# A graph-attention megakernel: first neighbour sweep inside the making of h, staggered tile pairs, scaling on ScalarE, mask conversion on GpSimd, weights loaded first

## The chip, the cores and the metric

The kernel runs on one core of a Trainium2 chip. The metric is device time in microseconds (us), here the median of three runs. TensorE is PE, VectorE is DVE, ScalarE is ACT, GpSimd is POOL, and SyncE (SP) issues most DMAs. An engine works through its own instructions in order and meets the others only through semaphores.

## The reference

Two graph layers follow each other, each with a residual and a layer norm, on x of 8 batches (B) x 2048 nodes (N) x 64 features (D); adj is a 2048 x 2048 matrix of 0 and 1.

```
h = einsum('bnf,of->bno', inp, W_w) + W_b ; h[:, 0] = 0
mask = (adj[1:, :] > 0)
neigh = einsum('ji,bjf->bif', mask, h[:, :N-1])
s = einsum('bif,fi->bi', h, a[:64]) + einsum('bif,fi->bi', neigh, a[64:]) ; s[:, 0] = 0
x1 = layernorm(x + leaky(s[:, :, None] * h.sum(1)[:, None, :]))
...
scores = where(adj + eye > 0, h1 @ h1.T, -1e16) ; softmax(scores) @ h1      (4 heads, then once more)
```

So the first layer needs one masked product over all nodes, and a scaling of each node; the second is dense attention, 8 x 4 instances of 2048 x 2048 in "layer 1" and 8 in "layer 2". The same adjacency serves both: as 0/1 for the product, and as 0/-1e16, with the diagonal at 0, for the attention.

## The kernel before

Everything is written out by hand with semaphores; each engine's program is its own function. Nodes go in 16 tiles (NT) of 128; one row of a tile holds 8 batches x 64 features = 512 columns. The part before the attention has these stages, in order:

- Loads. SP issues x in eight DMAs, then nine DMAs of weights and `a`, then two rows of adjacency tiles; the other adjacency tiles follow as their buffers come free.
- Weights. PE turns the weights and `a` (L642 to L651), DVE and ACT copy them out.
- Making of h, once per tile: POOL stages x (L570), PE transposes it (L661), ACT copies that (L893), PE multiplies it (L666), DVE adds the bias (L1024), takes the partial s (L1027, L1029), splits h into a high and a low part (L895 on ACT, L1032), and turns the adjacency integers into a 0/1 mask tile (L1036).
- The sum of h over all nodes: 32 matmuls (L673, L674), copied by ACT.
- Four neighbour sweeps on PE (L687, L688). A sweep makes 4 of the 16 output tiles in 4 PSUM banks from 16 x 4 x 2 matmuls of 512 columns. Tile 0 of the product uses a copy of h shifted by one node (`shifted`), which comes first in each sweep. Sweeps take turns on banks 0 to 3 and 4 to 7.
- Centring, on DVE, in pairs of tiles: eleven steps from the product (L1050) to the scaled result (L1086). In it DVE hands the centred values to ACT to be squared (L902), and the variance to POOL for the power -0.5 (L577), and waits for both before the scaling.
- Mask conversion on DVE: for each tile the diagonal (L1090) and then (m - 1) * 1e16 over 2048 columns (L1093).
- 32 units, each 4 tiles of one batch: POOL splits x1 (L586, L589), PE transposes (L704), ACT copies (L908), PE multiplies by the four heads (L724), ACT and DVE take the high and low parts (L920, L1103), PE turns them (L714), ACT and DVE copy (L913, L1098). SP stores `h_d` (L409) and `hT_d` (L413) to DRAM. A unit's buffers are those of the unit two before it, so L920 waits for that unit's store.
- Operand loads: SP waits for all stores, then loads the operands of attention instances 0 and 1 (L427, L423; 1.5 MB each). Then the attention starts (L819 on PE, L1160 on DVE).

The attention, from there to the end, is not touched by the change.

## Time and profile before

| what | value |
|---|---|
| median of 3 runs | 3358.05 us (3353.57 to 3359.98) |
| the profiled execution's own time | 3353.93 us |
| its span | 3352.2 us |
| PE, DVE, ACT, POOL busy | 91%, 83%, 70%, 75% |

The span is what the trace covers; 1.7 us lie around it. Busy shares are means over stages that are limited by different things, so the stages have to be read apart.

### The profile page before, as it was taken

Reading aid. Unit: us, or ns where it says so; the run is one execution under the profiler, and the core shown is the slowest. Engines: PE = TensorE matmul, PEld = TensorE weight load, DVE = VectorE, ACT = ScalarE, POOL = GpSimd, SP = SyncE. Lnnn points to the kernel's source line nnn. Section 1 sums busy time; section 2 is a strip of 40 time slices with the busy share of each in tenths; the row PEclk is TensorE's granted clock in tenths of the full one; section 3 lists DMA queues with packets and bytes.
Section 4 is the critical chain, followed back from the end, with each engine's and each line's share of the span. In section 5 each row is a group of like instructions: output and inputs, shape, how many; then the busy total and the mean of one; then the engine's idle time right before and its main releaser. Section 6 shows DMA issues by size and latency. Waiting matters only on the chain. (4 is left out here: it accounts for less than half of the span.)

```text
span 3352.2 us, 127058 instructions
## 1 busy us (share of the span) xinstructions
PE 3066.7 (91%) x49399; PEld 2295.4 (68%) x49399; DVE 2766.2 (83%) x5392; ACT 2336.7 (70%) x2678; POOL 2507.0 (75%) x1828
## 2 busy tenths in 40 slices
PE   3874599999999999999999999999996699999997
PEld 3433477777777777777777777777765577777775
DVE  5486488888888888888888888888876699999998
ACT  1104577777777777777777777777765588888886
POOL 1023189999999899999999999999986346676776
PEclk7887899999999999999999999999998899999998
DMA  5104879989999998999898899989966533333331
GB/s 205 66 0 150 285 134 164 164 154 170 167 156 161 165 164 157 161 166 161 156 170 166 156 163 167 161 158 174 163 124 209 189 123 125 118 135 119 134 120 73
DMA packets 1189157, 507.55 MB, mean 151 GB/s; under 512 B 1090718, under 2 KB 1148508, under 8 KB 1186588
## 3 DMA queue, kind: packets, MB, share of 16 engines
q1 hardware_dynamic: 1187564, 497.60, 69.9%
q8 instruction: 342, 5.60, 0.7%
q0 software_dynamic: 1200, 3.93, 0.3%
q14 instruction: 51, 0.42, 0.0%
HBM read 102.12 MB, written 62.91 MB: 49 GB/s over the span
## 5 line engine op out<-in xcount | busy, mean ns | idle before, releaser
L605 POOL TENSOR_TENSOR mask_slot<-probs 128x1024 f16<-128x1024 f32 x1024 | 1916.2, 1893 | 221.7 <-ACT probs L962 146.5
L962 ACT ACTIVATE probs<-scores,shifted_max 128x2048 f32<-128x2048 f32 x512 | 1026.1, 2004 | 177.0 <-DVE shifted_max L1165 172.9
L1160 DVE CUSTOM_DVE_ANT_0 scores<-ps,mask 128x1024 f32<-128x1024 f32 x512 | 625.8, 1222 | 206.6 <-PE ps L820 204.7
L819 PE MATMUL ps<-operands 128*128 128x512 f16 x2048 | 778.2, 380 | 12.4 <-DMA v_parts<-h_d 11.3
L820 PE MATMUL ps<-operands 128*128 128x512 f16 x2048 | 777.5, 380 | 0.0
L967 ACT COPY probsT<-ps 128x1024 bf16<-128x1024 bf16 x512 | 518.1, 1012 | 352.3 <-PE ps L828 352.3
L1160 DVE CUSTOM_DVE_ANT_0 scores<-ps,mask,neg_max 128x1024 f32<-128x1024 f32 x512 | 657.4, 1284 | 99.7 <-issue 52.8
L828 PEld LDWEIGHTS ps<-ident,probs 128*128 128x128 bf16 x8192 | 519.6, 98 | 291.9 <-issue 157.6
L828 PE MATMUL ps<-ident,probs 128*128 128x128 bf16 x8192 | 623.7, 219 | 5.8 <-DVE probsT L1169 3.6
L839 PE MATMUL ps<-v_parts,probsT 128*128 128x64 f16 x8192 | 548.0, 193 | 0.0
L838 PE MATMUL ps<-v_parts,probsT 128*128 128x64 f16 x8192 | 547.6, 193 | 0.0
L838 PEld LDWEIGHTS ps<-v_parts,probsT 128*128 128x128 bf16 x8192 | 512.5, 98 | 0.0
L839 PEld LDWEIGHTS ps<-v_parts,probsT 128*128 128x128 bf16 x8192 | 498.9, 98 | 0.0
L1169 DVE COPY probsT<-ps 128x1024 bf16<-128x1024 bf16 x512 | 354.0, 691 | 3.5 <-PE ps L828 3.4
L942 ACT ACTIVATE probsT<-ps 128x512 f16<-128x512 f32 x512 | 291.3, 595 | 78.1 <-PE ps L753 78.1
L811 PE MATMUL ps<-v_parts,probsT 128*128 128x64 f16 x8192 | 327.5, 193 | 15.7 <-DMA probsT<-mask_slot 9.9
L1129 DVE SCALAR_TENSOR_TENSOR probsT<-ps,probsT 128x512 f16<-128x512 f32 x512 | 329.4, 684 | 12.0 <-ACT probsT L942 3.5
L753 PE MATMUL ps<-ident,probs 128*128 128x128 f32 x2048 | 299.7, 279 | 5.8 <-DVE probsT L1129 4.7
L819 PEld LDWEIGHTS ps<-operands 128*128 128x128 f16 x2048 | 200.7, 98 | 136.6 <-DMA v_parts<-h_d 11.6
L811 PEld LDWEIGHTS ps<-v_parts,probsT 128*128 128x128 f16 x8192 | 276.0, 98 | 20.2 <-DMA probsT<-mask_slot 12.4
L820 PEld LDWEIGHTS ps<-operands 128*128 128x128 f16 x2048 | 200.7, 98 | 121.6 <-issue 1.1
L753 PEld LDWEIGHTS ps<-ident,probs 128*128 128x128 f32 x2048 | 226.7, 141 | 74.9 <-ACT probs L938 40.2
(169 smaller groups left out, 4545.2 us busy)
## 6 DMA issues: line engine op xcount, KB each, us to landing
mask_slot<-mask SPq DMA_DIRECT2D x129, 512.0 KB, 2.9
operands<-hT_d SPq DMA_DIRECT2D x40, 512.0 KB, 4.2
operands<-hT_d SPq DMA_DIRECT2D x80, 256.0 KB, 4.0
v_parts<-h_d SPq DMA_DIRECT2D x40, 512.0 KB, 4.6
scores<-in_adj SPq DMA_DIRECT2D x16, 1024.0 KB, 4.8
h_d<-probs SPq DMA_DIRECT2D x32, 512.0 KB, 3.5
hT_d<-probs SPq DMA_DIRECT2D x32, 512.0 KB, 2.8
probsT<-mask_slot SPq DMA_TRANSPOSE x1024, 3.5
```

The costliest lines, as they stand in the source:

```text
L605: pool.tensor_tensor(low[:, u, w], probs[:, u, w], high[:, u, w], ALU.subtract).then_inc(sem(f"low{half}"), 1)
L753: last = pe.matmul(ps[:, TURN_BANK[q], j * P:(j + 1) * P], probs[:, slot, c * P:(c + 1) * P], ident[:, :], start=(j == 0), stop=(j == 3), ...
L811: added = pe.matmul(out_slot(tt), lowT[:, u, c * P:(c + 1) * P], v_parts[:, held, c * P:c * P + D], start=False, stop=(c == NT - 1))
L819: pe.matmul(ps[:, b, :], hi_lo[:, p, t * P:(t + 1) * P], hi_lo[:, p, w], start=True, stop=False)
L820: scored = pe.matmul(ps[:, b, :], hi_lo[:, p, t * P:(t + 1) * P], lo_hi[:, p, w], start=False, stop=True)
L828: flipped = pe.transpose(high_bank(half)[:, j * P:(j + 1) * P], high[:, u, key:key + P], ident16[:, :])
L838: pe.matmul(out_slot(tt), w, v_parts[:, held, c * P:c * P + D], start=(c == 0), stop=False)
L839: added = pe.matmul(out_slot(tt), w, v_parts[:, held, c * P + D:(c + 1) * P], start=False, stop=False)
L962: act.activation(probs[:, 1 - u, :], scores[:, 1 - u, :], ACT.Exp, bias=shifted_max[:, 1 - u:2 - u], scale=-1.0, accum_out=row_sum[:, held ...
L967: act.copy(highT[:, u, N // 2:N], high_bank(1)).then_inc(sem("high_copied1"), 1)
L1160: dve.tensor_tensor_reduce(scores[:, u, w], ps[:, 2 * c:2 * c + 2, :].rearrange("p a n -> p (a n)"), mask[:, t * N + c * 2 * BANK:t * N + ...
L1169: dve.tensor_copy(highT[:, u, 0:N // 2], high_bank(0)).then_inc(sem("high_copied0"), 1)
```

## The change

Five edits, all ahead of the attention:

1. SP issues the nine weight DMAs before the eight of x.
2. PE's first sweep is spread over the making of h: the products of tile t-1 follow the making of h of tile t. The shifted tile now comes last in every sweep. The loops are written out.
3. DVE's pairs of tiles are staggered: the squares' sum and the variance of a pair are taken in the middle of the next pair. For this the centred values take turns between two buffers. The final scaling leaves DVE: ACT does it as eight activations of 64 columns for each tile (`normalize`).
4. The mask conversion goes from DVE to POOL, one tile after each second unit (`mask_step`); the diagonal is now a multiplication by `off_diagonal` after the conversion.
5. SP loads the operands of instance 0 before the last four units' stores, and those of instance 1 behind these stores; the waits for the stores move in part to ACT's first two exponentials.

```diff
@@ sync
-            for b in range(B):
-                sp.dma_start(xs[:, b * NT * D:(b + 1) * NT * D],
-                             x[b].rearrange("(p t) c -> p (t c)", t=NT)).then_inc(sem("x_loaded"), 16)
             sp.dma_start(w_nat[0:D, 0:D], w0).then_inc(sem("weights_loaded"), 16)
...
+            for b in range(B):
+                sp.dma_start(xs[:, b * NT * D:(b + 1) * NT * D],
+                             x[b].rearrange("(p t) c -> p (t c)", t=NT)).then_inc(sem("x_loaded"), 16)
...
+            with sp.Fori(0, B - 1) as b:
+                serve_units(b)
...
+            for u in range(2):
+                sp.wait_ge(sem(f"h_stored{u}"), 8 * (UNITS - NT // G))
+                sp.wait_ge(sem(f"hT_stored{u}"), 8 * (UNITS - NT // G))
+            for k in range(OPERAND_DMAS):
+                load_part(0, 0, k)
+            serve_units(B - 1)
+            for k in range(OPERAND_DMAS):
+                load_part(1, 1, k)
@@ gpsimd
-            units(pool, part_step)
+            def mask_step(t):
+
+                m = col(mask, t, N)
+                pool.tensor_scalar(m, m, -1.0, MASKED_SCORE, ALU.add, ALU.mult).then_inc(sem("mask_scaled"), 1)
+                pool.wait_ge(sem("mask_scaled"), t + 1)
+                gate(pool, "pool")
+                d = mask[:, t * (N + P):t * (N + P) + P]
+                pool.tensor_tensor(d, d, off_diagonal[:, :], ALU.mult).then_inc(sem("mask_ready"), 1)
+
+            for t in range(NT):
+                part_step(2 * t, 0)
+                part_step(2 * t + 1, 1)
+                mask_step(t)
@@ tensor
+            make_h(0, 0)
+            make_h(1, 1)
+            for t in range(2, NT):
+                make_h(t, t % 2)
+                products_of(0, 0, t - 1, t == 2)
+            products_of(0, 0, NT - 1, False)
...
+            products_shifted(0, 0, False).then_inc(sem("neigh_ready"), 1)
             pe.wait_ge(sem("hsum_copied"), 1)
...
+            for sweep in range(1, 4):
+                u = sweep % 2
+                if sweep >= 2:
+                    pe.wait_ge(sem("neigh_free"), 4 * (sweep - 1))
+                for t in range(1, NT):
+                    products_of(sweep, u, t, t == 1)
+                products_shifted(sweep, u, False).then_inc(sem("neigh_ready"), 1)
@@ scalar
+            def normalize(i):
+                sm = small[:, :, i % 2 * B:(i % 2 + 1) * B]
+                act.wait_ge(sem("a_rstd"), i + 1)
+                for b in range(B):
+                    scaled = act.activation(x_btc[:, b, i, :], pair(centred(i))[:, b, :], ACT.Copy, scale=sm[:, 3, b:b + 1])
+                scaled.then_inc(sem("x1_done"), 1)
@@ vector
+                if i0:
+                    for i in (i0 - 2, i0 - 1):
+                        spread(i)
+                    for i in (i0 - 2, i0 - 1):
+                        variance(i)
...
-                        dve.tensor_tensor(x_btc[:, :, i, :], pair(w[:, 2, :]), over(sm[:, 3, :]), ALU.mult).then_inc(sem("x1_done"), 1)
-
-            with dve.Fori(0, NT) as t:
-                d = mask[:, bass.ds(t * (N + P), P)]
-                dve.tensor_tensor(d, d, ident16[:, :], ALU.max).then_inc(sem("mask_diag"), 1)
-                dve.wait_ge(sem("mask_diag"), t + 1)
-                m = mask[:, bass.ts(t, N)]
-                dve.tensor_scalar(m, m, -1.0, MASKED_SCORE, ALU.add, ALU.mult).then_inc(sem("mask_ready"), 1)
```

On POOL, at the start of the units, before the change (L591 makes the bias rows, L586 and L589 split one unit's x1; the row behind the first four is the loop's branch):

```order
L591 COPY operands<-bh_rows 128x2048
L586 CAST scores<-xs 128x4x64
L589 TENSOR_TENSOR scores<-xs,scores 128x4x64
L586 CAST scores<-xs 128x4x64
L589 TENSOR_TENSOR scores<-xs,scores 128x4x64
L174 UNCONDITIONAL_BRANCH
```

The same place of the changed kernel (L602 and L605 are the split, L612 the conversion of one mask tile, L616 its diagonal):

```order
L607 COPY operands<-bh_rows 128x2048
L602 CAST scores<-xs 128x4x64
L605 TENSOR_TENSOR scores<-xs,scores 128x4x64
L602 CAST scores<-xs 128x4x64
L605 TENSOR_TENSOR scores<-xs,scores 128x4x64
L612 TENSOR_SCALAR mask<-mask 128x2048
L616 TENSOR_TENSOR mask<-mask,off_diagonal 128x128
L602 CAST scores<-xs 128x4x64
L605 TENSOR_TENSOR scores<-xs,scores 128x4x64
```

Two instructions on the mask now stand between each second unit and the next, 16 times over.

On PE, in the making of h, before the change (L661 transposes x, L666 multiplies it):

```order
L661 MATMUL ps<-ident,probsT 128x128 x4
L666 MATMUL ps<-w0T,outs 128x128 x4
L659 REGISTER_ALU
L661 MATMUL ps<-ident,probsT 128x128 x4
L666 MATMUL ps<-w0T,outs 128x128 x4
```

And of the changed kernel (L688 and L693 are the same two steps, L701 and L702 the products of the sweep with h's high and low part):

```order
L688 MATMUL ps<-ident,probsT 128x128 x4
L693 MATMUL ps<-w0T,outs 128x128 x4
L701 MATMUL ps<-probs,mask 128x512
L702 MATMUL ps<-operands,mask 128x512
L701 MATMUL ps<-probs,mask 128x512
L702 MATMUL ps<-operands,mask 128x512
L701 MATMUL ps<-probs,mask 128x512
L702 MATMUL ps<-operands,mask 128x512
L701 MATMUL ps<-probs,mask 128x512
L702 MATMUL ps<-operands,mask 128x512
L688 MATMUL ps<-ident,probsT 128x128 x4
L693 MATMUL ps<-w0T,outs 128x128 x4
```

Eight products of 512 columns now stand between two tiles' transposes.

## Rows read from the trace of the kernel before

**Rows 1.** Busy time in stretches: length, then engines, granted clock, DMA share, GB/s.
```profile
29.50:122.00 92.50, 50.32 (x225) 38.89 (x226) 72.53 (x80) 19.79 (x33) 13.47 (x15) 0.65 0.48 162
149.70:268.00 118.30, 82.78 (x384) 37.35 (x382) 95.11 (x193) 9.85 (x16) 25.96 (x16) 0.86 0.00 0
288.20:405.50 117.30, 74.82 (x868) 62.15 (x868) 58.41 (x65) 74.07 (x91) 28.77 (x54) 0.95 0.79 279
418.00:2555.00 2137.00, 2101.68 (x37028) 1565.90 (x37026) 1804.60 (x3727) 1601.47 (x1549) 1930.02 (x1030) 0.99 0.90 160
```

**Rows 2.** Timeline, loads' end and first tile: start, length, engine, line, idle before.
```profile
14.21 0.61 POOL L570 COPY probsT<-xs 128x512 f32 x1 [11.06 <-DMA xs<-in_x]
22.73 0.28 PE L642 MATMUL ps<-ident,scratch 64*64 64x64 f32 x1 [22.73 <-DMA rows<-in_L_gnn_beta]
29.58 1.00 PE L661 MATMUL ps<-ident,probsT 128*128 128x128 f32 x4 [2.44 <-ACT probsT L886]
...
31.25 2.08 PE L666 MATMUL ps<-w0T,outs 128*128 128x128 f32 x8 [0.68 <-ACT outs L893]
```

**Rows 3.** Timeline of the making of h.
```profile
55.57 1.16 PE L666 MATMUL ps<-w0T,outs 128*128 128x128 f32 x8 [2.09 <-ACT outs L893]
...
98.65 0.68 DVE L1024 TENSOR_TENSOR mask_slot<-ps,rows 128x512 f32<-128x512 f32 x1
...
100.72 2.08 PE L666 MATMUL ps<-w0T,outs 128*128 128x128 f32 x8 [2.09 <-ACT outs L893]
...
103.67 0.69 DVE L1024 TENSOR_TENSOR mask_slot<-ps,rows 128x512 f32<-128x512 f32 x1
```

**Rows 4.** Timeline of the four sweeps, first and last of 512 matmuls.
```profile
121.81 0.39 PE L687 MATMUL ps<-operands,mask 128*128 128x512 f16 x1 [1.20 <-ACT hsum L898]
...
232.10 0.38 PE L688 MATMUL ps<-operands,mask 128*128 128x512 f16 x1
```

**Rows 5.** Timeline of the end of the last pair's centring.
```profile
261.68 0.69 DVE L1075 SCALAR_TENSOR_TENSOR mask_slot<-small,mask_slot 128x512 f32<-128x512 f32 x1
...
264.09 3.24 POOL L577 TENSOR_TENSOR small<-small,half_neg 128x8 f32<-128x8 f32 x2 [11.52 <-DVE small L1082]
265.75 0.69 DVE L1086 TENSOR_TENSOR xs<-probsT,small 128x512 f32 x1 [1.80 <-POOL small L577]
267.36 0.69 DVE L1086 TENSOR_TENSOR xs<-mask_slot,small 128x512 f32 x1 [0.91 <-POOL small L577]
```

**Rows 6.** Timeline of the units' first and last steps, and the attention's first.
```profile
268.12 1.89 POOL L591 COPY operands<-bh_rows 128x2048 f32<-128x2048 f32 x1 [0.79 <-DVE xs L1086]
...
274.99 1.01 ACT L920 CAST probs<-ps 128x1024 f16<-128x1024 f32 x1 [1.98 <-PE ps L724]
...
288.23 2.35 DVE L1103 TENSOR_TENSOR probs<-ps,probs 128x1024 f16<-128x1024 f32 x2
...
400.69 1.22 DVE L1103 TENSOR_TENSOR probs<-ps,probs 128x1024 f16<-128x1024 f32 x1 [2.31 <-ACT probs L920]
...
402.66 1.86 PE L714 MATMUL ps<-ident_h,probs 128*128 128x128 f16 x16 [3.08 <-DVE probs L1098]
...
418.04 1.22 DVE L1160 CUSTOM_DVE_ANT_0 scores<-ps,mask 128x1024 f32<-128x1024 f32 x1 [12.79 <-PE ps L820]
```

**Rows 7.** Waits in the first 420 us: total, times, longest.
```profile
ACT probs L920 <- DMA h_d<-probs: 31.3, 26, 1.6
```

**Rows 8.** Groups of instructions by form: busy, mean ns, idle before.
```profile
L589 POOL TENSOR_TENSOR scores<-xs,scores 128x256 f16<-128x256 f16 x28 | 19.2, 685 | 5.1 <-POOL scores L586 5.1
...
L356 POOL TENSOR_SCALAR scratch<-outs 128x512 f32<-128x512 f32 x15 | 28.9, 1924 | 3.1 <-POOL outs L354 3.1
...
L354 POOL TENSOR_TENSOR outs<-outs,rows 128x512 f32<-128x512 f32 x15 | 19.1, 1277 | 2.7 <-POOL outs L353 2.7
...
L951 ACT ACTIVATE outs<-ps 128x64 f32 x93 | 20.8, 223 | 19.6 <-PE ps L767 19.6
...
L340 POOL TENSOR_SCALAR stats<-stats 128x8 f32<-128x8 f32 x30 | 5.9, 198 | 5.8 <-POOL stats L334 5.8
```

More of the change, by code:

```diff
@@ L63, in build @@
         ident16 = sb("ident16", [P, P], BF16)
+        off_diagonal = sb("off_diagonal", [P, P], BF16)
         ident_h = sb("ident_h", [P, P], F16)
@@ new lines, in products @@
+            def products(sweep, u, t, hi, lo, start, stop):
+                for j in range(4):
+                    m = mask[:, t * N + sweep * (4 * P) + j * P:t * N + sweep * (4 * P) + (j + 1) * P] if isinstance(t, int) else \
+                        mask[:, bass.ds(t * N + (sweep * (4 * P) + j * P), P)]
+                    pe.matmul(ps[:, 4 * u + j, :], m, hi, start=start, stop=False)
+                    last = pe.matmul(ps[:, 4 * u + j, :], m, lo, start=False, stop=stop)
+                return last
@@ new lines, in products_of, with products_shifted @@
+            def products_of(sweep, u, t, start):
+                pe.wait_ge(sem("mask_made"), t + 1)
+                if sweep == 0:
+                    pe.wait_ge(sem("lo_made"), t)
+                products(sweep, u, t, col(h_hi, t - 1, BD), col(h_lo, t - 1, BD), start, False)
+            def products_shifted(sweep, u, start):
+                return products(sweep, u, 0, shifted[:, 0:BD], shifted[:, BD:2 * BD], start, True)
+            make_h(0, 0)
[3 more added lines that the diff above has]
+                products_of(0, 0, t - 1, t == 2)
@@ L1095, in copy_hT @@
+            for i in (NT - 2, NT - 1):
+                spread(i)
+            for i in (NT - 2, NT - 1):
+                variance(i)
             def copy_hT(k, u):
```

169 lines of the change are left out of this document (79 added, 90 removed).

## The prediction

> **What bounds the kernel now.** I first read busy times by stretch [rows 1]. From 418 to 2555 us is the first attention layer, PE busy 2102 of 2137 us; the change does not touch it, nor what follows. All edits fall before 418 us, so the question is by how much the first attention step, DVE's L1160 at 418.04 [rows 6], moves. Then I read the timeline at each junction there, asking which engine has no gaps. In the making of h, DVE is busy 72.5 of 92.5 us while PE is at clock 0.65 on average [rows 1]; a tile takes DVE 5.02 us, from one L1024 to the next [rows 3]. The four sweeps run without a gap: 511 steps in 110.3 us, 0.216 us each, 27.6 us a sweep [rows 4]. DVE can't start centring before the first is through, then needs 118.3 us for 8 pairs, 14.8 each [rows 1], so the other three hide behind it. In the units no engine is full; ACT's L920 waits 31.3 us in 26 times for a store [rows 7], and a unit takes 117.3 / 32 = 3.67 us [rows 1]. POOL has 28.8 us of work there, in 54 instructions, so 1.07 us a unit [rows 1].
>
> I write times on the clock of the trace before.
>
> **Weights first.** x lands at 14.2, all weights at 22.7; PE then needs 6.9 us for weights and `a` before the first transposes at 29.6 [rows 2]. With the weights in front, their chain runs while x still arrives, and the start hangs on x: POOL's copy, 0.61, then PE. x is there at 22.7 at the latest (before, everything had landed by then): transposes at 23.4, gain 6.2. At best the weights, a third of x's bytes or less, cost 3.5 us more than x's 14.2: gain 11. I take x at 20.5, gain 8.3.
>
> **First sweep in the making of h.** In order, PE now does transposes of t, waits for ACT's copy, multiplies, then does 8 products of tile t-1 once DVE has made that mask tile, which is at the end of its 5.02 us. At full clock, from then on: 8 x 0.216 = 1.7, transposes at most 1.0 and the copy 0.68 [rows 2], multiplication 1.16 [rows 3]: 4.6 us, below 5.02, so DVE stays the bound and the products cost nothing. The cover is 0.4 us thin. At half the clock (L666 2.08 in place of 1.16 [rows 3]) it is 3.45 + 1.0 + 0.68 + 2.08 = 7.2 us, and 0.2 of handing over: 2.4 us more a tile. PE starts there cold; I charge 2 us for the first such tile, and expect full clock after, since PE would be over nine tenths busy at the half clock and 70% at the full one, while the units' stage holds 0.95 with 74.8 of 117.3 us busy, 64% [rows 1].
>
> The last mask tile is made at 103.67 + 2 x 5.02 = 113.7 [rows 3]. Then 8 products (1.7), the 32 matmuls of the sum of h (6.9) and 8 products of the shifted tile (1.7): DVE can start at 124.1 instead of 149.7. With 8.3 gained above and 2 paid: 117.9.
>
> **Staggered pairs.** A pair loses the two waits for POOL, 1.80 and 0.91 [rows 5], the two scalings (start to start 0.60 each) and about 0.2 of waiting for the square: 14.8 becomes 10.7. Two pairs, 21.4 us, now fit under a sweep of 27.6, so PE bounds: 117.9 + 3 x 27.6 = 200.7. Behind the last sweep come two pairs, 21.4, to 222.1. What is late next is the tail: from the end of the last L1075 (262.37) to the end of the powers (267.33), 5.0 us [rows 5], then ACT's eight scalings of the last tile at 0.223, the nearest row (L951, out of PSUM [rows 8]): 1.8. ACT's other scalings hide under DVE's pairs: 16 x 0.223 + 2 x 0.63 = 4.8 of 10.7 us. x1 is complete at 228.9, against 268.05 before: 39 us gained.
>
> **Mask conversion on POOL.** DVE loses the wait till 288.23 for L1103, whose input was there at 276.0 (L920, 274.99 + 1.01) [rows 6]. POOL gets, after each second unit, one TENSOR_SCALAR with two operations over 2048 columns. No row has this in bf16. The nearest is L356, the same instruction with two operations, 512 columns in 1.924 us, and L340 with 8 columns in 0.198 [rows 8]: 1.726 / 504 = 3.42 ns a column, so 0.2 + 2040 x 0.00342 = 7.2 us. From below it is bounded by the copy of 2048 columns, 1.89 [rows 6]; from above by twice the slowest two-input rate, L354, (1.277 - 0.198) / 504 = 2.14 ns, twice that over 2040 columns: 8.9. I take 7.2: same engine, same form. L356 repeats at 1.92 in 15 places, so no neighbour makes it slow. With the diagonal (0.45; 256 columns take 0.685 [rows 8]) and a wait of 0.18, a mask step is 7.8 us, and a round of two units and a mask tile 2 x (1.07 + 0.18) + 7.8 = 10.3 us. The units want 2 x 3.67 = 7.3. **So POOL becomes the bound of this stage**, behind it PE's L704, which waits for the split, and everything after. This eats most of the gain.
>
> POOL starts 1.96 after x1 is complete (L591 ends at 270.01 [rows 6]): 230.9. The split of unit 30 ends at 230.9 + 15 x 10.3 + 1.25 = 386.7, the last mask tile at 395.7. From the split of unit 30: 4.6 to its L1103 (as at the first unit: 276.1, less 271.5 for the split's end), 3.7 to that of unit 31, 3.8 to the end of L714 (400.69 to 404.52 [rows 6]), 2.2 to DVE's first step (four matmuls and the start), and 1.5 for a cold PE: 15.8. L1160 starts at 402.5 in place of 418.04.
>
> **Operands early.** The 12.8 us for which DVE waited before L1160 [rows 6] go; that is in the line above. In the units SP loads 1.5 MB more, at 279 GB/s [rows 1] 5.4 us; in rounds of 10.3 us there is room for it. ACT's waits for the last stores fall into the first steps of the attention; behind them are only exponentials whose inputs are not yet there.
>
> **Sum.** 418.0 - 402.5 = 15.5 us off the profiled execution's own 3353.9: 3338.4. That execution lies 4.1 below the median of 3358.05, so a median could be 3342.5. I predict 3341.
>
> **Rivals.**
>
> *POOL's conversion is quick, and all the gain stays.* From a mask instruction of 4.2 us down, the round is under 7.3 and the stage keeps its 3.67 a unit. Then L1103 starts at 228.9 + 8.0 = 236.9, that of unit 31 at 236.9 + 31 x 3.67 + 1.5 = 352.2, and SP's early loads now do cost their 5.4 (nothing at least; up to 9, when the wait for the landed stores adds to it): 357.6; 6.0 on to L1160: 363.6, a gain of 54.4: 3299.5 to 3303.7. For it: L591, 2048 columns with one input in 1.89. Against it: L356, and that its minimum is no obviously dearer operation than an addition. Chance 0.22. The Trainium skill (GPSIMD Engine Reference, Engine selection) says that one-input elementwise work is roughly at line rate on GpSimd; by that the conversion would take about what L591 takes, and this rival would be the result. L356 in this trace disagrees with it, and I go by the trace.
>
> *In between*, 4.2 to 6.4 us an instruction: each microsecond is 16 us of time, 3304 to 3328. Chance 0.14.
>
> *TensorE stays at half clock while h is made* (slower). Place: PE between two mask tiles. Price 2.4 us x 14 tiles = 34 us, less the 2 charged: 3341 + 32 = 3373. It takes 9 cold tiles to turn my forecast into a loss above 0.2%. For it: the clock is 0.65 in this stage now [rows 1]. Against it: PE's share rises well over what the units' stage holds its clock with. Chance 0.07.
>
> *POOL's conversion is dearer than L356 tells*, bf16 in and out costing more: from 8.6 us on the kernel is slower by more than 0.2%; at 8.9 it is 3368. Chance 0.07.
>
> My forecast, 6.4 to 8 us, has 0.50; its own range is 3328 to 3354.
>
> **How the numbers follow.** 0.2%, 6.7 us, is about what a measurement of this kernel can tell from no change. The two upper cases hold 0.14, the lower ones 0.36; a range of 3297 to 3358 leaves out most of the upper two and the very bottom. Faster: 0.22 + 0.14 and all but the upper edge of the forecast, 0.78. Within 0.2%: an instruction of 7.8 to 8.6 us, or a few cold tiles: 0.11. Slower: 0.11.
>
> **What would show it.** After: the first transposes near 21 us; DVE's centring starting near 118, PE's three sweeps without a gap, DVE waiting for them; x1 complete near 229. Then POOL without gaps through the units, the mask's TENSOR_SCALAR at 7.2, rounds of 10.3, PE's L704 waiting for POOL, L1160 near 402. Wrong if that instruction is under 4.2 us (then the stores bound the units, and L1160 is near 364), or if granted clock in the making of h stays near 0.5 and DVE waits for PE there.

## The result, and the profile after

The changed kernel took 3320.16 us (median of 4 runs, 3313.20 to 3323.41); the kernel before took 3355.81 beside it (4 runs). The ratio is 0.9888, with a 95% interval of 0.9872 to 0.9903: about 36 us less, where the prediction had 17. The profiled execution took 3323.41 us, of which 3321.7 are its span. DVE's first attention step, `tensor_tensor_reduce` of the scores, is now L1217 (it was L1160 [rows 6]; L1160 now is the remainder of a unit, which was L1103). It moved from 418.04 to 375.22, by 42.8 us; the prediction had it at 402.5.

Busy time of the changed kernel in the stretches that answer to [rows 1]: length, then the engines, granted clock, DMA share, GB/s.

```profile
25.10:119.00 93.90, 64.42 (x310) 39.41 (x311) 75.71 (x80) 20.69 (x32) 15.15 (x15) 0.85 0.49 169
128.90:232.00 103.10, 82.73 (x384) 37.30 (x382) 80.62 (x172) 33.48 (x121) 27.63 (x14) 0.92 0.00 1
249.00:370.00 121.00, 74.05 (x851) 61.10 (x852) 55.84 (x61) 73.05 (x92) 64.89 (x89) 0.94 0.77 269
```

The third row is the one to read first. The prediction made POOL the bound of the units; it is busy 64.9 of 121 us there. This is the row of the mask's instruction (count, shortest/median/longest in ns, first and last start), and under it POOL's timeline through one round of two units and a mask tile:

```profile
L612 POOL TENSOR_SCALAR mask<-mask x16: 1895/1897/1899, 245.8 to 351.8; 128x2048 bf16<-128x2048 bf16 x16
```
```profile
285.80 1.90 POOL L612 TENSOR_SCALAR mask<-mask 128x2048 bf16<-128x2048 bf16 x1
287.88 0.43 POOL L616 TENSOR_TENSOR mask<-mask,off_diagonal 128x128 bf16<-128x128 bf16 x1 [0.18 <-POOL mask L612]
288.25 0.40 POOL L602 CAST scores<-xs 128x256 f16<-128x256 f32 x1
...
291.93 0.40 POOL L602 CAST scores<-xs 128x256 f16<-128x256 f32 x1 [2.43 <-PE ps L744]
...
293.14 1.90 POOL L612 TENSOR_SCALAR mask<-mask 128x2048 bf16<-128x2048 bf16 x1
```

1.90 us and not 7.2. A round takes 293.14 - 285.80 = 7.3 us, which is what two units want, and POOL waits 2.4 us of it for PE.

The start. Timeline of the changed kernel at the loads' end (answers to [rows 2]), then its first 24 us in two stretches (columns as above):

```profile
13.86 0.28 PE L670 MATMUL ps<-ident,scratch 64*64 64x64 f32 x1 [13.86 <-DMA rows<-in_L_gnn_beta]
24.37 0.61 POOL L587 COPY probsT<-xs 128x512 f32 x1 [20.82 <-DMA xs<-in_x]
25.13 1.09 PE L688 MATMUL ps<-ident,probsT 128*128 128x128 f32 x4 [6.91 <-POOL probsT L587]
```
```profile
2.00:14.00 12.00, 0.14 (x1) 0.13 (x1) 0.17 (x1) 0.14 (x1) 1.33 (x6) 1.00 0.61 181
14.00:24.40 10.40, 4.21 (x23) 3.39 (x22) 3.77 (x10) 2.05 (x4) 0.03 (x1) 0.83 1.03 421
```

The weights are there 9 us earlier, but x 10 us later. The first transposes gain 29.58 - 25.13 = 4.4 us, where 8.3 were predicted: while the weights come, DMA moves 181 GB/s, and x only then runs at 421.

The centring. DVE's last mask tile and its first centring step (answers to [rows 4]), then the end of the centring and the first unit (answers to [rows 5, 6]):

```profile
114.84 1.86 DVE L1090 TENSOR_SCALAR mask<-scores 128x2048 int32 x1
128.86 0.69 DVE L1114 TENSOR_TENSOR probsT<-ps,probsT 128x512 f32<-128x512 f32 x1 [12.16 <-PE ps L702]
```
```profile
234.06 0.69 DVE L1101 TENSOR_REDUCE small<-probsT 128x8 f32<-128x512 f32 x1 [1.81 <-ACT probsT L952]
...
235.49 3.23 POOL L593 TENSOR_TENSOR small<-small,half_neg 128x8 f32<-128x8 f32 x2 [4.14 <-DVE small L1106]
237.16 3.93 ACT L943 ACTIVATE xs<-outs,small 128x64 f32<-128x64 f32 x16 [2.62 <-POOL small L593]
241.15 1.89 POOL L607 COPY operands<-bh_rows 128x2048 f32<-128x2048 f32 x1 [2.42 <-ACT xs L943]
248.98 1.23 DVE L1160 TENSOR_TENSOR probs<-ps,probs 128x1024 f16<-128x1024 f32 x1 [13.44 <-ACT probs L972]
```

Centring starts 20.9 us earlier than before (31.9 predicted), x1 is complete at 241.1, 27 us earlier (39 predicted), and the first remainder of a unit 39.3 us earlier: the other 12 us come from DVE, which no longer stands before it with the mask.

The end of the units. SyncE's timeline, and ACT's and DVE's there:

```profile
356.54 1.90 SPq L435 DMA_DIRECT2D operands<-hT_d  x3
358.50 0.56 SPq L431 DMA_DIRECT2D v_parts<-h_d  x1
359.12 0.42 SPq L415 DMA_DIRECT2D h_d<-probs  x1
```
```profile
366.51 1.01 ACT L972 CAST probs<-ps 128x1024 f16<-128x1024 f32 x1 [9.20 <-DMA h_d<-probs]
...
371.04 1.22 DVE L1160 TENSOR_TENSOR probs<-ps,probs 128x1024 f16<-128x1024 f32 x1 [1.66 <-ACT probs L972]
...
375.22 1.22 DVE L1217 CUSTOM_DVE_ANT_0 scores<-ps,mask 128x1024 f32<-128x1024 f32 x1 [0.43 <-PE ps L860]
```

The new place of a cost: SyncE loads instance 0 ahead of the last four units' stores, and ACT waits 9.2 us for one of these. From the first remainder to the last it takes 122.1 us, 9.6 more than before (288.23 to 400.69 [rows 6]). In return DVE no longer waits 12.8 us before the attention.

Theory: the mechanism was right, and the price of one instruction, the mask conversion, was wrong; two smaller sizes (the start, and the making of h with the sweep inside) were wrong on the other side. Rival: the mask's price matters little, because something else (buffers between POOL and PE, transfers) sets the units' pace anyway; and the gain comes from other edits.

### The profile page after: what moved, and what is told of

It is laid out like the page before. It is cut to its first block and busy times, and to the rows that moved or that the text cites. A ratio compares the mean times of both kernels' runs of the same rounds, so it can differ in the third digit from the quotient of the medians.

```text
span 3321.7 us, 126248 instructions
## 1 busy us (share of the span) xinstructions
PE 3065.0 (92%) x49399; PEld 2287.0 (69%) x49399; DVE 2739.8 (82%) x5344; ACT 2369.3 (71%) x2806; POOL 2546.0 (77%) x1861
## 5 line engine op out<-in xcount | busy, mean ns | idle before, releaser
L1217 DVE CUSTOM_DVE_ANT_0 scores<-ps,mask 128x1024 f32<-128x1024 f32 x512 | 625.5, 1222 | 202.4 <-PE ps L860 196.5
L1217 DVE CUSTOM_DVE_ANT_0 scores<-ps,mask,neg_max 128x1024 f32<-128x1024 f32 x512 | 657.3, 1284 | 103.4 <-issue 57.7
L851 PEld LDWEIGHTS ps<-v_parts,probsT 128*128 128x128 f16 x8192 | 275.7, 98 | 25.9 <-DMA probsT<-mask_slot 21.0
```

Of the source, the lines that this page charges most:

```text
L851: added = pe.matmul(out_slot(tt), lowT[:, u, c * P:(c + 1) * P], v_parts[:, held, c * P:c * P + D], start=False, stop=(c == NT - 1))
L1217: dve.tensor_tensor_reduce(scores[:, u, w], ps[:, 2 * c:2 * c + 2, :].rearrange("p a n -> p (a n)"), mask[:, t * N + c * 2 * BANK:t * N + ...
```

## The experiments

Stage times below are starts of the first attention step unless said otherwise; in the changed kernel it is 375.2, and 375.6 in a second profile of it (`a0_after_again`, below), so differences are taken to 375.4. Apart from the changed kernel and `c2_together`, every variant was executed once.

**What made the nearest row dear.** Ahead of POOL's wait for x, seven instructions by themselves:

```diff
+            for o, i, c1, c2, op1, op2 in ((wide, wide, -1.0, 2.0, ALU.add, ALU.mult), (wide, wide, 0.0, -0.8, ALU.min, ALU.mult),
+                                           (flat, src, -1.0, 2.0, ALU.add, ALU.mult), (flat, src, 0.0, -0.8, ALU.min, ALU.mult),
+                                           (flat, src, 0.0, -0.8, ALU.max, ALU.mult), (flat, src, -0.8, None, ALU.mult, None),
+                                           (flat, src, 0.0, None, ALU.min, None)):
```

> The changed kernel, and ahead of it, while GpSimd has nothing to do but wait for x, seven TENSOR_SCALAR on GpSimd over buffers that are rewritten later: two over 2048 bf16 columns (add then multiply; minimum then multiply) and five over 512 fp32 columns (add, multiply; minimum, multiply; maximum, multiply; multiply alone; minimum alone). The mask's instruction took 1.897 us for 2048 bf16 columns, the row that I had priced it from, minimum and multiply over 512 fp32 columns, 1.924. Theory A, the minimum is what is slow: 2048 bf16 with minimum about 7 us, 512 fp32 with add about 0.5 us and with minimum 1.9. Theory B, fp32 is what is slow: both wide bf16 ones 1.9 us, all two-operation fp32 ones 1.9. Theory C, it was slow because VectorE worked at the same time: all of 512 columns near 0.5 us here, where VectorE is idle.

The seven in their order (L593 is the call with one operation; count, shortest/median/longest in ns, start):

```profile
L595 POOL TENSOR_SCALAR mask<-mask x1: 1899/1899/1899, 5.9 to 5.9; 128x2048 bf16<-128x2048 bf16 x1
L595 POOL TENSOR_SCALAR mask<-mask x1: 7095/7095/7095, 7.9 to 7.9; 128x2048 bf16<-128x2048 bf16 x1
L595 POOL TENSOR_SCALAR scratch<-outs x1: 620/620/620, 15.0 to 15.0; 128x512 f32<-128x512 f32 x1
L595 POOL TENSOR_SCALAR scratch<-outs x1: 1920/1920/1920, 15.7 to 15.7; 128x512 f32<-128x512 f32 x1
L595 POOL TENSOR_SCALAR scratch<-outs x1: 1925/1925/1925, 17.7 to 17.7; 128x512 f32<-128x512 f32 x1
L593 POOL TENSOR_SCALAR scratch<-outs x1: 1506/1506/1506, 19.7 to 19.7; 128x512 f32<-128x512 f32 x1
L593 POOL TENSOR_SCALAR scratch<-outs x1: 1490/1490/1490, 21.3 to 21.3; 128x512 f32<-128x512 f32 x1
```

Theory A. The same 2048 columns of bf16 take 1.90 us with add and multiply and 7.10 with minimum and multiply: the prediction's 7.2 was right for an instruction that the kernel does not issue. The type is not what decides: 512 fp32 columns take 0.62 with add and multiply, and 1.92 with minimum or maximum, as in [rows 8]. Nor is VectorE: it was idle during the instruction of 7.10 us but for 0.2 us. (It was at work from 15.4 to 19.4, beside the two of 1.92, so these two alone would not show that.) What nobody expected: one operation alone, a multiplication or a minimum, takes 1.5 us, so the pair of add and multiply is the cheap case, not the addition. The constants were changed together with the operations (a factor of 2.0 behind the addition, -0.8 in the other products); that they play no part was not tried by itself.

**The price as predicted, put into the kernel.**

```diff
-                pool.tensor_scalar(m, m, -1.0, MASKED_SCORE, ALU.add, ALU.mult).then_inc(sem("mask_scaled"), 1)
-                pool.wait_ge(sem("mask_scaled"), t + 1)
-                gate(pool, "pool")
+                for again in range(4):
+                    pool.tensor_scalar(m, m, -1.0 if again == 3 else 0.0, MASKED_SCORE if again == 3 else 1.0,
+                                       ALU.add, ALU.mult).then_inc(sem("mask_scaled"), 1)
+                    pool.wait_ge(sem("mask_scaled"), 4 * t + again + 1)
+                    gate(pool, "pool")
```

> The changed kernel with GpSimd's mask conversion made as dear as the prediction took it to be: the 2048 columns are first rewritten three times by the same instruction with 0 added and a factor of 1, so four instructions of 1.9 us, 7.6, stand where one stood. Theory A (the price of that instruction is the one step that failed, and the rest of the chain holds): GpSimd is without gaps, a round of two units takes 2 x 1.25 + 7.6 + 4 x 0.18 + 0.43 = 11.3 us, and the first attention step is at 243 + 15 x 11.3 + 1.25 + 15.8 = 429.5. Rival (the buffers between GpSimd and TensorE let the units run on while a mask is converted): the rounds take no more than the 8.5 us of the added instructions and one unit, the first attention step is under 400.

Measured 429.7, and 3368.68 us for the execution, beside 3359.03 of the kernel before. POOL's timeline, from one round's first conversion to the next round's:

```profile
301.13 1.90 POOL L613 TENSOR_SCALAR mask<-mask 128x2048 bf16<-128x2048 bf16 x1
...
307.40 1.90 POOL L613 TENSOR_SCALAR mask<-mask 128x2048 bf16<-128x2048 bf16 x1 [0.19 <-POOL mask L613]
309.48 0.43 POOL L618 TENSOR_TENSOR mask<-mask,off_diagonal 128x128 bf16<-128x128 bf16 x1 [0.18 <-POOL mask L613]
...
312.25 1.90 POOL L613 TENSOR_SCALAR mask<-mask 128x2048 bf16<-128x2048 bf16 x1
```

A round of 11.1 us without a gap (11.3 expected), and the first attention step within 0.2 us of the place that the prediction's chain gives (429.5). That it is so close is in part luck: the rounds take 2.7 us less than the chain has, the stretch from the split of unit 30 (its end at 411.6) to the first attention step 18.1 us where it has 15.8. The rival of this section falls: POOL's price does set the pace once it is over what two units want.

**Each edit undone by itself.** The diffs are the reverse of the change's: `u1` issues x before the weights, `u2` puts the products of sweep 0 behind the sum of h, `u3` brings VectorE's waits and scalings back into each pair, `u4` brings the loop over the mask tiles back to VectorE (ahead of the units), `u5` puts the loads of instances 0 and 1 behind all stores:

```diff
@@ u2_sweep_apart, tensor
                 make_h(t, t % 2)
-                products_of(0, 0, t - 1, t == 2)
-            products_of(0, 0, NT - 1, False)
...
+            for t in range(1, NT):
+                products_of(0, 0, t, t == 1)
             products_shifted(0, 0, False).then_inc(sem("neigh_ready"), 1)
@@ u5_operands_late, sync
-            for u in range(2):
-                sp.wait_ge(sem(f"h_stored{u}"), 8 * (UNITS - NT // G))
-                sp.wait_ge(sem(f"hT_stored{u}"), 8 * (UNITS - NT // G))
-            for k in range(OPERAND_DMAS):
-                load_part(0, 0, k)
             serve_units(B - 1)
-            for k in range(OPERAND_DMAS):
-                load_part(1, 1, k)
...
+            for i in range(2):
+                for k in range(OPERAND_DMAS):
+                    load_part(i, i, k)
```

> The changed kernel with the first edit undone: x's eight loads are issued before the nine of the weights again. Theory A (the edit is worth what the trace shows, 4.4 us at the first transposes): first transposes at 29.6 in place of 25.1, first attention step at 375.2 + 4.4 = 379.6. Rival (something later, the adjacency's arrival or the clock, takes up what the start gives): first transposes 4.4 later, the first attention step under 2 us later.

> The changed kernel with the second edit undone: the products of sweep 0 stand behind the sum of h as a sweep of their own, and none within the making of h. Theory A (that sweep's 27.6 us less the shifted tile's part are hidden in the making of h, at the price of a few cold tiles): the centring starts at 128.9 + 16.5 = 145.3, x1 is complete 16.5 later, at 257.6, the first attention step at 391.7. Rival (TensorE, cold and waited for in the making of h, makes the interleaving cost more than the 3 us that its mask tiles end late): without it the making of h ends by 112 instead of 116.7, and the first attention step is under 388.

> The changed kernel with the third edit undone: VectorE waits for square and power within each pair of tiles and scales itself. Theory A: a pair takes 14.8 us again, two of them 29.6, just over a sweep's 27.6, so VectorE is the bound from 128.9 on: x1 is complete at 128.9 + 118.3 = 247.2 in place of 241.1, the first attention step at 381.3. Rival (TensorE's sweeps bound the centring either way): x1 is complete within 2 us of 241.1, or earlier, since two scalings on VectorE end before sixteen on ScalarE.

> The changed kernel with the mask conversion back on VectorE, between the centring and the units; GpSimd only splits x1. Theory A (the conversion on GpSimd is hidden, and was worth VectorE's delay alone): VectorE converts from 235.5 to about 255.5, so the first remainder of a unit starts there in place of 248.98, and the first attention step at 375.2 + 6.5 = 382. Rival (GpSimd's 37 us among the units slow them): the units go faster by more than that, and the first attention step is at 375 or earlier.

> The changed kernel with the fifth edit undone: the operands of instances 0 and 1 are loaded when all stores have landed. Theory A (the early load costs ScalarE 9.2 us of waiting for a store, and saves the 13 us of loading at the end): the last remainder starts 9 us earlier, about 362, the first attention step 17.3 behind it, 379.3, 4 us later than with the edit. Rival (the units are bound by the bytes, so the wait is only moved): the last remainder 5 us earlier, the first attention step at 383.

| run | first transposes | centring starts | last remainder | first attention step | edit is worth | execution (median for the first row) |
|---|---|---|---|---|---|---|
| changed kernel | 25.1 | 128.9 | 371.0 | 375.2 | | 3320.2 |
| u1_weights_last | 29.8 | 132.3 | 374.1 | 379.7 | 4.3 | 3326.8 |
| u2_sweep_apart | | 144.6 | 387.8 | 392.0 | 16.6 | 3335.7 |
| u3_scale_on_dve | | 129.7 | 374.6 | 380.4 | 5.0 | 3331.2 |
| u4_mask_on_dve | 25.2 | 128.3 | 377.1 | 382.9 | 7.5 | 3326.9 |
| u5_operands_late | 25.3 | 128.2 | 362.6 | 380.6 | 5.2 | 3339.7 |

The five sum to 38.6 us of 42.8. The first attention step came within 1.3 us of theory A's number in all five, in `u3` by luck: x1 is complete at 244.6, between A's 247.2 and the rival's 243, and the clock added 1.6 us at the end.

Not all of the column "edit is worth" is the edit's. Two stretches of the path are set by TensorE, through the same instructions in all the runs named here, and their length goes with its granted clock. From the start of the last mask tile to the centring it is 12.6 us at clock 1.00 (`w1`, `p5` below), 13.9 to 14.3 at 0.88 (the changed kernel, `u1`, `u3`, `u4`, `u5`), and 15.5 at 0.78 (`p1`, `p2`, `p6`). From the last remainder to the first attention step it is 4.2 us in both profiles of the changed kernel and in `u2`, and 5.6 to 5.9 in `u1`, `u3` and `u4`. Length, PE's work, clock and so on of this last stretch, the changed kernel first, `u1` second:

```profile
371.04:375.22 4.18, 2.84 (x29) 1.89 (x28) 2.51 (x3) 2.02 (x2) 0.00 (x0) 0.84 0.89 314
374.06:379.67 5.61, 4.27 (x29) 2.84 (x28) 2.51 (x4) 2.02 (x2) 0.00 (x0) 0.56 0.93 330
```

Ahead of it PE waited 9 us for ACT in both and then ran at half the clock in both; why its next instructions, 1.3 us behind these, run at the full clock in one trace and at half in the other was not found. So about 1.5 us of what the table gives for `u1`, `u3` and `u4` can't be put down to the edit from one trace each. At the last remainder they are worth 2.8, 3.3 and 5.8 (against 371.3, the mean of two profiles), and the five sum to 34 to 39. Each does something; that they add up to 42.8 is not shown more closely than that.

In `u2` the rival had half a point, and it is the prediction's second failed size. The rows of the 0/1 mask instruction in the making of h (busy us, mean ns, idle before), the changed kernel first, `u2` second:

```profile
L1090 DVE TENSOR_SCALAR mask<-scores 128x2048 int32 x16 | 32.6, 2035 | 0.0
```
```profile
L1090 DVE TENSOR_SCALAR mask<-scores 128x2048 int32 x16 | 30.2, 1885 | 0.0
```

Without the interleaving the last mask tile is done at 109.6 instead of 116.7. Of these 7 us, 2.4 are in this row, 0.4 in the row above it (L1086), and 4.1 are waits of VectorE for PE's L693 (13.7 in all, 9.6 of them the start, which `u2` has too). All of the 4.1 stand behind stretches at half clock: 2.3 at 46.5, and 0.9 at 84.7 and at 101.4, where the eight products of a tile had just run at a granted clock of 0.50 (79.0 to 82.0 and 95.9 to 98.6). The mean of 2035 ns mixes two lengths: ten of the sixteen take 1.86 to 1.90 us, as all do in `u2`, and six take 2.29 to 2.30. The six are the ones that start 0.5 us into GpSimd's copy of a tile of x (L587), and that copy takes 1.05 us instead of 0.61. The first two rows are such a pair; in the next two the copy starts later, and the mask instruction keeps its length:

```profile
54.23 1.05 POOL L587 COPY probsT<-xs 128x512 f32 x1 [2.16 <-PE ps L688]
54.72 2.29 DVE L1090 TENSOR_SCALAR mask<-scores 128x2048 int32 x1
98.55 1.88 DVE L1090 TENSOR_SCALAR mask<-scores 128x2048 int32 x1
99.74 1.17 POOL L587 COPY probsT<-xs 128x512 f32 x1 [6.07 <-PE ps L688]
```

PE's products are not beside the slow ones: the next begin at 57.07, when the mask instruction is done, and none are running at 54.72. What the interleaving changes is when PE releases GpSimd's copy, and the copy is what VectorE meets. In `u5` PE waits 12.1 us for `v_parts` ahead of the attention, which is the wait of before come back.

**The clock in the making of h.** Work for TensorE that nobody reads, put where it would wait:

```diff
+            def warm(n):
+                for k in range(n):
+                    pe.matmul(ps[:, 3, :], ident[:, :], a_in[:, k * 512:(k + 1) * 512], start=True, stop=True)
...
+            warm(4)
             make_h(0, 0)
+            warm(2)
             make_h(1, 1)
+            warm(2)
             for t in range(2, NT):
                 make_h(t, t % 2)
+                if t == 2:
+                    warm(1)
```

> The changed kernel with work for TensorE that nobody reads: four fp32 matmuls of 512 columns while it waits for x, two behind tile 0, two behind tile 1 and one behind tile 2 of the making of h. Theory A (it is the half clock of the first tiles, 0.50 from 22 to 34 and from 38 to 46 us, which lets VectorE wait 2.3 us at 46.5 and stretches the first tiles): clock near 1 from 25 us on, the wait gone, the centring starts at 125 to 126.5 in place of 128.9, the first attention step 2.5 to 3.5 earlier. Rival (what stretches the making of h is VectorE itself, its mask instruction at 2.29 in place of 1.89 beside GpSimd's copy): clock up, centring start within 1 us of 128.9.

Busy time and clock of the first tiles, the changed kernel first, `w1` second:

```profile
26.00:34.00 8.00, 6.04 (x25) 5.06 (x24) 4.48 (x5) 1.78 (x3) 1.55 (x2) 0.50 0.15 62
34.00:46.00 12.00, 7.29 (x28) 4.51 (x28) 9.20 (x11) 2.50 (x4) 1.36 (x2) 0.64 0.59 185
```
```profile
26.00:34.00 8.00, 6.65 (x35) 4.16 (x33) 5.16 (x6) 1.90 (x3) 1.23 (x2) 1.00 0.17 70
34.00:46.00 12.00, 7.79 (x43) 4.49 (x42) 10.71 (x13) 3.23 (x5) 1.96 (x2) 1.00 0.59 190
```

The clock goes from 0.50 and 0.64 to 1.00, VectorE does more in each stretch, the centring starts at 125.9 (3.0 earlier) and the attention at 373.1 (2.3 earlier). Theory A in the numbers, but only half of the 3.0 comes from the first tiles. There, VectorE's wait of 2.3 us at 46.5 is gone, as expected; the added matmuls themselves move the first transposes from 25.1 to 25.9, and the last mask tile starts 1.5 earlier (113.4). The other 1.5 is the clock of 1.00 instead of 0.88 behind the last mask tile, which `p5` below has too without any such work. Of the 7 us the later waits are still there, now three of 0.9 us, and so are the long mask instructions: seven of 2.29 us, each 0.5 us into a copy of GpSimd that takes 1.05. Its one execution took 3308.12 us, 12 less than the changed kernel; all but 2.3 of that lies behind the first attention step (2933 us from there to the end, the shortest of all traces), and no run ties that to the warm start.

**What the start hangs on.** Two other orders of the first loads:

```diff
@@ p1_weights_by_act
-            sp.dma_start(w_nat[0:D, 0:D], w0).then_inc(sem("weights_loaded"), 16)
...
+            act.dma_start(w_nat[0:D, 0:D], w0).then_inc(sem("weights_loaded"), 16)
...
@@ p2_order, sync: w0, wh, wo, a, b0, then x, then two adjacency tiles, then
+            sp.dma_start(bh_rows[:, :, :].rearrange("p h d -> p (h d)"),
+                         bh.rearrange("h d -> (h d)").rearrange("(o n) -> o n", o=1).to_broadcast([P, H * D])).then_inc(sem("rows_loaded"), 16)
+            for k, row in enumerate((bo, gamma, beta)):
+                sp.dma_start(rows[:, 1 + k, :], row.rearrange("(o c) -> o c", o=1).to_broadcast([P, D])).then_inc(sem("rows_loaded"), 16)
```

> The changed kernel with the nine weight loads issued by ScalarE, beside x's eight by SyncE, in place of one row. Theory A (the loads queue behind one another at the one issuing engine: weights first let x land at 24.4, x first let the weights land at 22.7 with x at 14.2): both have landed by 17 us, the first transposes are at 22 (PE's 6.9 us for weights, then the first tile), 3 earlier, and so is the first attention step, 372. Rival (the transfers share the DMA engines, busy share 1.03 from 14 us on, and small weight packets crowd x): x lands at 22 or later, the first transposes at 24 to 26, no gain.

> The changed kernel with another order of SyncE's first loads: the three weight matrices, a and b0 (1.2 MB), then x, then two adjacency tiles, and last the rows that the making of h does not need (bh, bo, gamma, beta), with a semaphore of their own that GpSimd waits for before the bias rows. Theory A (with the weights first, the slow ones are the row loads, at 85 to 200 GB/s, and x, 4.2 MB at 420 GB/s in 10 us, queues behind them): x has landed by 17 to 18.5, the first transposes are at 18 to 20 in place of 25.1, and the first attention step 5 to 7 us earlier, 369. Rival (x's time is set by bytes, 1.2 and 4.2 MB at 420 GB/s after a start at 2, and a alone is slow): x at 21 or later, under 3 us gained.

The first row is x's landing and the second the first transposes, in `p1`, and then in `p2`:

```profile
19.74 0.61 POOL L577 COPY probsT<-xs 128x512 f32 x1 [16.19 <-DMA xs<-in_x]
...
30.92 0.63 PE L678 MATMUL ps<-ident,probsT 128*128 128x128 f32 x4 [2.19 <-issue]
```
```profile
20.64 0.61 POOL L588 COPY probsT<-xs 128x512 f32 x1 [17.09 <-DMA xs<-in_x]
...
21.39 1.09 PE L690 MATMUL ps<-ident,probsT 128*128 128x128 f32 x4 [6.22 <-POOL probsT L588]
```

`p1` missed both of its theories: x lands at 19.7 but the last weight row only at 23.9, so PE starts its weights then, and the first attention step is at 383.5, 8 us later (1.5 of it the clock behind the last mask tile, 1.6 that behind the last remainder). The two issuing engines share the DMA engines (share 0.95 from 2 to 10 us), and the weights take longer among x's packets: the last row 18.4 us from issue to landing, where it took 8.3 ahead of x. The Trainium skill (DMA: Bandwidth & Descriptors, Issuing engines are not separate DMA queues) says just that, DMAs of different issuers run on the same 16 engines and interleave; this trace agrees.

`p2` lies between its theories: 3.7 us gained at the first transposes (5 to 7 expected under A, under 3 under the rival). The slow rows were one part; the other is bytes, `a` alone being 1 MB. At the attention only 0.6 of it was left (374.8). The last mask tile still started 4.5 earlier (110.4); then the clock took 1.5 back before the centring (0.78 instead of 0.88) and 1.5 behind the last remainder (5.7 us instead of 4.2), and the units 1.4 (123.5 us from the first remainder to the last, against 122.1). Only what happened among the units was not found.

**The wait for the store at the end of the units.** `p5` loads one of the eight operand parts behind every second unit's stores from the 16th unit on; `p6` only drops SyncE's wait:

```diff
@@ p5_loads_spread, sync
+            for b in range(B // 2, B):
+                serve_units(b, lambda k, b=b: load_part((b - B // 2) // 2, (b - B // 2) // 2, (b - B // 2) % 2 * 2 + k))
@@ p6_no_wait_landed, sync
-            for u in range(2):
-                sp.wait_ge(sem(f"h_stored{u}"), 8 * (UNITS - NT // G))
-                sp.wait_ge(sem(f"hT_stored{u}"), 8 * (UNITS - NT // G))
```

> The changed kernel with the operand loads of instances 0 and 1 spread: one of the eight parts behind every second unit's stores, from the 16th unit on, with no wait of SyncE for landed stores (both instances come out of the first four units, stored long before). Theory A (the 9.2 us in which ScalarE waits near the end come from SyncE, which holds the last units' stores behind a wait for landed ones and a bunch of loads): that wait goes; 3 MB more in 16 units cost at most 3 of them back; the last remainder starts at 362 to 366 in place of 371.0, and the first attention step at 367 to 370 in place of 375.2. Rival (the units are bound by bytes: 292 GB/s at a share of 0.83): 3 MB take 10 us wherever they stand, the last remainder stays at 371 or goes up, the first attention step is at 374 or later.

> The changed kernel without SyncE's wait for the landed stores of 28 units before the loads of instance 0 (which come out of the first four units); the loads stay where they are, ahead of the last four units' stores. Theory A (the 9.2 us in which ScalarE waits are this wait's 2 to 4 us and 1.5 MB of loads, 5.4 us): the wait falls to about 6, the first attention step 3 earlier, 372.5. Rival (bytes alone: the stores in flight have to pass anyway before the loads do): within 1 us of 375.4.

Theory A fell in both, and the rivals' numbers came. With the loads spread, ACT's longest wait for a store is 4.8 us instead of 9.2, yet the last remainder is at 371.2 and the first attention step at 377.2. Without the wait it is 7.5 us at the most, and 375.1. From the first remainder to the last the units take 114.3 us with no early load (`u5`), 121.2 with 1.5 MB and no wait (`p6`), 122.1 with 1.5 MB and the wait, 123.6 with 3 MB spread (`p5`). At 269 GB/s (the row of 249 to 370) 1.5 MB would take 5.6 us and 3 MB 11.2; they cost 7 to 8 and 9.3. So it is mostly the bytes, and SyncE's wait is 1 us of it at the most; why a bunch costs more for each byte than spread loads is not shown. The 377.2 of `p5` is not the loads': it runs from the last remainder to the attention at clock 0.50, in 6.0 us instead of 4.2. The early load moves 3 MB out of the gap before the attention, where `u5` needs 18.1 us from the last remainder to the attention, and half of it into a stage in which stores set the pace; that is why it is worth 5 and not the 12.8 of the wait that it removed.

**Does the attention pay back?** The span fell by 30.5 us only, where the first attention step moved 42.8; from there to the end it took 2934.2 us before and 2946.5 after. Both kernels once more, unchanged:

> The kernel before, unchanged, profiled once more, to see how far layer 1 of the attention, which the change does not touch, varies by itself. From the first L1160 to the last it took 2097.5 us in the first trace; the four traces of the changed kernel and its variants so far have 2104.1 to 2116.4 there, 7 to 19 us more, which is half of what the change gained ahead of the attention (42.8) and lost again (12.3) by the end. Theory A (scatter of an execution and of a chip, whatever the kernel): this run has 2103 or more too. Rival B (the changed kernel enters the attention in another phase, or its code lies elsewhere, and pays for it in all 32 instances): this run has 2098 again, within 2 us.

> The changed kernel once more, unchanged, for a second profile of it. In the first, from the first attention step to the end it was 2946.5 us; the kernel before had 2934.2 in one profile and 2942.2 in another. Theory A (scatter, whatever the kernel): this one lies anywhere in 2934 to 2948. Rival B (something in the changed program costs the attention some 6 us each time): 2944 or more again.

DVE's first instruction of layer 1, first and last start, in the first and second profile of the kernel before (L1160), then of the changed one (L1217):

```profile
L1160 DVE CUSTOM_DVE_ANT_0 scores<-ps,mask x512: 1210/1225/1227, 418.0 to 2515.5; 128x1024 f32<-128x1024 f32 x171
```
```profile
L1160 DVE CUSTOM_DVE_ANT_0 scores<-ps,mask x512: 1207/1225/1227, 419.5 to 2525.4; 128x1024 f32<-128x1024 f32 x171
```
```profile
L1217 DVE CUSTOM_DVE_ANT_0 scores<-ps,mask x512: 1207/1225/1226, 375.2 to 2483.2; 128x1024 f32<-128x1024 f32 x171
```
```profile
L1217 DVE CUSTOM_DVE_ANT_0 scores<-ps,mask x512: 1210/1225/1226, 375.6 to 2477.6; 128x1024 f32<-128x1024 f32 x171
```

The same kernel needs 2097.5 or 2105.9 us before, 2108.0 or 2102.0 after: theory A, scatter, in both. In the second pair 43.9 us at the attention's start are 43.2 in the span. From the first attention step to the end, the two profiles of before have 2934 and 2942 us, the 15 of the changed kernel and its variants 2933 to 2957, 2944 on the mean with a deviation of 6. These traces alone leave room for a systematic loss between none and more than 12 us. The medians of four are sharper: they fell by 35.7 us (32.5 to 43 by the interval), the first attention step by 43.3 on the mean of both pairs. By this estimate the changed kernel loses some 8 us from there on, 0 to 11 within the interval; what takes them was not found. `u5` is the far end, 2957, and its execution of 3339.68 us the longest of the five `u` runs, though its first attention step is only 5.2 late; whether that is scatter was not repeated.

**The parts together.** The order of loads of `p2`, the warm start, no wait before instance 0's loads, and the last tile scaled by VectorE:

```diff
             normalize(NT - 2)
-            normalize(NT - 1)
...
+            dve.wait_ge(sem("a_rstd"), NT)
+            dve.wait_ge(sem("a_centred"), NT)
+            dve.tensor_tensor(x_btc[:, :, NT - 1, :], pair(centred(NT - 1)), over(small[:, 3, B:2 * B]), ALU.mult).then_inc(sem("x1_done"), 1)
```

> The changed kernel with four things together: the order of loads of p2_order, the warm start of TensorE, no wait of SyncE for landed stores before instance 0's loads, and the last tile's scaling on VectorE (one instruction of 0.6) beside ScalarE's eight for the tile before. Theory A (all lie on the one path to the first attention step and add up): 6 from the loads, 2.5 from the clock, 2 from the last scaling, 0 to 3 from the wait: the first attention step at 362 to 366 in place of 375.4, the ratio to the kernel before 0.9855 +- 0.0015. Rival (the attention's own scatter or a later bound hides them): 0.988 or more.

3306.9 us (median of 5, 3301.08 to 3307.59), ratio to the kernel before 0.9843, interval 0.9824 to 0.9863: better than both kernels, with an interval apart from the change's. The ratio is where theory A had it (0.9855 +- 0.0015), the first attention step is not: it is at 368.1, short of the 362 to 366 hoped for, as `p2` and `p6` by themselves let expect. The centring starts 5.1 earlier (123.8), the first remainder 7.0 (242.0), the last 7.0 (364.0). Of the 13.3 us between the two medians only these 7 are accounted for; the other 6 lie behind the first attention step, in the attention's own scatter or the loss above.

## Why the prediction was wrong in size and right in direction

- *Weights first*: "I take x at 20.5, gain 8.3". x landed at 24.4 and the gain was 4.4 (below the 6.2 given as the least). The step that failed is "the weights, a third of x's bytes or less, cost 3.5 us": it counted bytes, and the row loads ran at half the rate (181 GB/s up to 14 us). `p2_order` shows 3.7 us of it to be the order.
- *First sweep in the making of h*: that it hides was right (centring 16 us later without it), the charge of 2 us was too small: 7 us. Of these 4.1 are waits behind the half clock, at one tile of the start (2.3, where 2.4 was reckoned for such a tile) and at two later ones (0.9 each), and 2.8 are VectorE's own instructions, which get longer where they meet GpSimd's copy and for which the prediction had no term. The rival of a cold TensorE in all tiles did not come: 0.95 from 46 to 80 us, 0.92 from there to the last mask tile, with two tiles at 0.50.
- *Staggered pairs*: PE bounds the three sweeps, VectorE waiting for it, as said. From centring to x1 complete it took 112.2 us, predicted 111.0. ACT's scaling takes 332 ns and not 223, but eight of them follow each other in 2.0 us, predicted 1.8.
- *Mask conversion on POOL*: "That is 7.2 us". This is the step that failed. The instruction takes 1.90, the lower bound that was given; the rival "POOL's conversion is quick" is what happened. Its chain then ends within 0.6 us: it puts the first attention step at 363.6 with x1 complete at 228.9; with the measured 241.1 this is 375.8, and 375.2 was measured. That is closer than its terms are. From the first remainder to the last it has 120.7, with SyncE's early loads at 5.4, and 122.1 was measured; from there to the attention it has 6.0, and 4.2 was measured, with TensorE's clock at 0.84, where it was 0.53 in the same place before. The rule of the Trainium skill that the prediction set against the row (GPSIMD Engine Reference, Engine selection) was right for this instruction, 1.90 beside the copy's 1.89, and `m1_pool_forms` shows where it does not hold: 7.10 with a minimum.
- *The two misses had opposite signs.* With x1 at 241.1, the forecast's own chain from there (402.5 - 228.9 = 173.6) would have ended at 414.7, hardly a gain; `x4_mask_four_times` shows that chain to hold at about its price. The mask's price gave 39 us back.

## What to carry to other kernels

The nearest row must have the same operations, not only the same engine and form: on GpSimd the pair of operations decided by a factor of 3.7, while type and neighbours did not matter. Where one unknown price carries the sum and the bounds lie 4 to 1 apart, the prediction is a choice between cases; the lower bound, a plain copy of the same width, deserved as much weight as the dearer relative. A single trace decides between edits only down to what the clock does at the junctions: here 1.5 us at each of two, with the same instructions before and behind, so look at the granted clock of every stretch that one engine passes alone before calling a difference the edit's. A load moved ahead of others costs them its time at its own rate, so price it from GB/s in that stretch and not from bytes; and bytes moved out of a gap into a stage that transfers already bound come back as waits there.

## What was not expected of the hardware

- GpSimd's TENSOR_SCALAR on 512 fp32 columns: 0.62 us with add and multiply, 1.92 with minimum or maximum and multiply, 1.50 with one operation alone, multiplication included. The single operation is dearer than the pair.
- VectorE's mask instruction (int32 to bf16, 2048 columns) takes 1.86 to 1.90 us, but 2.29 where it starts 0.5 us into a copy by GpSimd, and that copy takes 1.05 instead of 0.61: six times in the changed kernel, seven in `w1_warm_start`, never in `u2_sweep_apart`, where the two do not meet. What the two share was not tried.
- The same PE instructions between the last remainder and the attention take 4.2 us at a granted clock of 0.84 or more and 5.6 to 6.0 at 0.50 to 0.56. Both occur among variants of one kernel, and what decides was not found.
- The last of the nine weight loads landed 10 us later when ScalarE issued them beside x's eight than when SyncE issued them ahead of x (23.9 against 13.8).
